# The orders of all five engines made anew in a transformer block of two gated FFNs around an attention step

## The reference

```python
x = x + 0.5 * ffn(layernorm(x))
x = x + attn(layernorm(x))
x = x + 0.5 * ffn(layernorm(x))

# ffn, hidden width 512, weights w*, h* ternary (-1, 0, 1)
h = silu(x @ w1.T * w1_s) * (x @ w2.T * w2_s)
h = gelu(h @ h1.T * h1_s)
h = gelu(h @ h2.T * h2_s)
y = h @ w3.T * w3_s

# attn, with a second layer norm of its own (gamma, beta)
keys = h @ Wk.T + bk;  values = h @ Wv.T + bv
w = exp((keys @ Wka.T + bka) / sqrt(128))
w = w / cumsum(w, axis=1)
out = cumsum(w * keys, axis=1) * values
```

## Time and profile before

| what | us |
|---|---|
| median of 3 runs (range) | 367.62 (367.56 to 367.99) |
| span of the profiled execution | 366.2 |
| median less that span (start and end outside it) | 1.4 |
| PE busy | 359.0 (98% of the span) |
| DVE busy | 319.5 (87%) |
| ACT busy | 283.6 (77%) |
| POOL busy | 171.9 (47%) |

### The profile page before, as it was taken

One profiled execution on the slowest core, in us unless ns is written; L12 is line 12 of the kernel. 1 busy time (PEld: TensorE's weight loads), 2 busy tenths in 40 slices (PEclk: granted clock), 3 DMA queues, 4 the chain that ended last, 5 costly groups with the idle time before them and its releaser, 6 DMA issues.

```text
span 366.2 us, 5192 instructions
## 1 busy us (share of the span) xinstructions
PE 359.0 (98%) x1572; PEld 284.6 (78%) x1572; DVE 319.5 (87%) x542; ACT 283.6 (77%) x463; POOL 171.9 (47%) x259
## 2 busy tenths in 40 slices
PE   7999999999999999999999999999999999999995
PEld 2678888778877887887878787887878877888885
DVE  5999788989989989999999989999999799947742
ACT  5898777886897789777876969868888796777763
POOL 3583375694124578512794545663574740520000
PEclk9999999999999999999999999999999999999999
DMA  7725504042000302100221021022024010050001
GB/s 255 242 96 167 166 2 115 0 113 62 1 2 0 99 18 58 59 4 0 56 63 57 3 58 59 0 59 58 0 60 117 1 57 2 0 143 2 30 1 59
DMA packets 17534, 21.44 MB, mean 59 GB/s; under 512 B 7392, under 2 KB 8672, under 8 KB 17248
## 3 DMA queue, kind: packets, MB, share of 16 engines
q1 hardware_dynamic: 16640, 20.15, 19.9%
q10 hardware_dynamic: 864, 0.93, 0.8%
HBM read 18.89 MB, written 2.19 MB: 58 GB/s over the span
## 4 chain that ended last, share of the span: by engine, by line
PE 97%; DVE 1%; ACT 0%; issue 0%; POOL 0%; POOLq 0%; DVEq 0%
PE hid_ps L654 62%; PE gate_ps L654 8%; PE y_ps L654 8%; PE up_ps L654 7%; PE y_ps L673 2%; PE xt_ps L847 2%; PE xt_ps L843 2%; PE xt_ps L850 2%; PE y_ps L763 1%; PE up_ps L718 1%; PE gate_ps L718 1%; DVE full L1092 0%; PE xt_ps L654 0%; DVE gate L1080 0%; DVE xt_sb L1152 0%
## 5 line engine op out<-in xcount | busy, mean ns | idle before, releaser
L654 PE MATMUL hid_ps<-act_hi,hi_h 128*128 128x512 f32 (+1 forms) x368 | 146.5, 398 | 0.0
L654 PE MATMUL hid_ps<-act_lo,hi_h 128*128 128x512 f32 (+1 forms) x368 | 143.1, 389 | 0.0
L1102 DVE TENSOR_TENSOR act_lo<-full,act_hi 128x512 fp32r<-128x512 f32 x157 | 117.3, 769 | 20.9 <-ACT act_hi L918 17.7
L911 ACT ACTIVATE full<-hid_ps,vec 128x512 f32<-128x512 f32 x123 | 84.3, 686 | 53.3 <-PE hid_ps L654 36.9
L654 PEld LDWEIGHTS hid_ps<-act_lo,hi_h 128*128 128x128 f32 x368 | 69.2, 188 | 16.3 <-issue 1.4
L654 PEld LDWEIGHTS hid_ps<-act_hi,hi_h 128*128 128x128 f32 x368 | 69.2, 188 | 16.0 <-issue 1.4
L918 ACT ACTIVATE act_hi<-full 128x512 fp32r<-128x512 f32 x127 | 78.6, 628 | 1.6
L580 POOL TENSOR_TENSOR xnt<-xt_sb,wide 128x512 f32<-128x512 f32 x22 | 31.6, 1437 | 49.5 <-DMA wide<-rows 43.8
L654 PE MATMUL hid_ps<-act_hi_second,hi_h 128*128 128x512 f32 x128 | 52.1, 407 | 0.0
L654 PE MATMUL hid_ps<-act_lo_second,hi_h 128*128 128x512 f32 x128 | 50.0, 390 | 0.0
L894 ACT ACTIVATE tanh<-gate_ps,s_half 128x512 f32<-128x512 f32 x60 | 40.6, 682 | 8.9 <-PE gate_ps L654 8.8
(11 more groups left out here) (168 smaller groups left out, 542.7 us busy)
## 6 DMA issues: line engine op xcount, KB each, us to landing
wide<-rows SPq DMA_DIRECT2D x44, 256.0 KB, 3.7
out<-xt_sb SPq DMA_DIRECT2D x7, 256.0 KB, 3.1
raw_h<-h2t SPq DMA_DIRECT2D x4, 256.0 KB, 7.0
x_sb<-x SPq DMA_DIRECT2D x1, 1024.0 KB, 5.0
xt_sb<-xt SPq DMA_DIRECT2D x1, 1024.0 KB, 5.0
x_sb<-x SPq DMA_DIRECT2D x3, 256.0 KB, 5.5
raw_h<-h1t SPq DMA_DIRECT2D x2, 256.0 KB, 6.0
xt_sb<-xt SPq DMA_DIRECT2D x2, 256.0 KB, 4.1
```

The costliest lines, as they stand in the source:

```text
L654: mm = eng.matmul(ps, w, a, start=(first and n == 0), stop=(last and n == len(seq_) - 1))
L911: eng.activation(full23[m % 2][:, :], home23(n, T, m)[:, :], ACT.Gelu, scale=col("sh1" if n == 2 else "sh2", m)).then_inc(s_gelu[n], 1)
L1102: eng.tensor_tensor(act_lo[a][:, m, :], full[m % 2][:, :], act_hi[a][:, m, :].bitcast(F32), ALU.subtract).then_inc(s_lo[n], 1)
```

## The change

Only the tables change. The same items stand in them, each exactly once: 286 on PE, 441 on DVE, 436 on ACT, 87 on POOL and 51 on SP. No function, buffer or semaphore is touched, and `PE` in `START` stays as it was. Strings are now longer or empty because an item's step number no longer follows its tile. The diff, cut to the head and three further places:

```diff
@@ -30,15 +30,18 @@
-        "hi:w1 bits:w2 hi:w2 z vec:s1 0:t bits:h1.1 bits:h1.3 0:tanh.0 0:tanh.1 0:tanh.2 0:high1.0 0:high1.1",
-        "bits:h2.0 bits:w3 tanh.3 high1.2 z.0 z.1 high1.3",
+        "hi:w1 bits:w2 hi:w2",
+        "0:z vec:s1 t bits:h1.1 tanh.0 tanh.1 bits:h1.3 bits:h2.0 tanh.2 high1.0 high1.1 tanh.3 bits:w3 "
+        "high1.2 z.0 z.1",
     ),
     "DVE": (
-        "stats aggr veps bits:w1 norm.0 norm.1 flag:copy1 norm.2 bits:h1.0",
-        "t vec:scales bits:h1.2 stats flag:raise2 gate.0 gate.1 up.0 flag:copy2 up.1 low1.0 aggr gate.2 veps "
-        "up.2 bits:h2.1 gate.3 up.3 2:stats low1.3 bits:h2.2 flag:raise3 1:t 3:stats flag:copy3 0:low2.0 "
-        "1:gate.0 0:low2.1 1:gate.1 1:up.0 1:up.1 0:low2.2 0:low2.3 1:low1.0 1:gate.2 1:low1.1 1:up.2 "
-        "1:gate.3 0:low3.0 2:t 1:up.3 1:low1.2 1:low1.3 0:low3.1 0:fold 0:low3.2",
+        "stats aggr veps bits:w1",
+        "0:norm.0 0:norm.1 0:norm.2 flag:copy1 bits:h1.0 vec:scales t bits:h1.2 stats gate.0 gate.1 "
+        "flag:raise2 up.0 flag:copy2 up.1 low1.0 aggr gate.2 veps up.2 gate.3 2:stats up.3 bits:h2.1 "
+        "bits:h2.2 low1.3 3:stats 1:t flag:raise3 flag:copy3 0:low2.0 0:low2.1 1:gate.0 1:gate.1 1:up.0 "
+        "1:up.1 0:low2.2 0:low2.3 1:low1.0 1:low1.1 1:gate.2 1:gate.3 1:up.2 1:up.3 0:fold 0:low3.0 0:low3.1 "
+        "2:t 1:low1.2 1:low1.3 2:gate.0 2:up.0 2:gate.1 0:low3.2 2:up.1 0:low3.3 1:low2.0 2:low1.0 2:low1.1 "
+        "2:gate.2 0:dt",
     ),
 }
 
@@ -46,143 +49,156 @@
 SECOND_LAYER = (
...
-    "p2dhi.1 p2bhi.2 p2dlo.1 p2dhi.2 p2dhi.3 flag:sum3 p1.0 p2dlo.2 p2dlo.3 p1.1"
+    "p2dhi.1 p2bhi.2 p2dlo.1 p2dhi.2 p2dhi.3 flag:sum3 p1.0 p1.1 p2dlo.2 p2dlo.3"
...
-        "park wide",
-        "park wide",
-        "a0:park a0:wide park wide",
-        "a1:park a1:wide park wide",
...
+        "park 3:park",
+        "",
+        "2:wide 3:wide a0:park",
...
-        "p1.0 p1.1 p4 p2.0 p2.1 u a4:values p2.2 p1.2 p2.3 a5:logits p1.3 12:u p3.0 a5:keys p3.1 p3.2 p3.3",
...
+        "a4:keys 10:p1.0 10:p1.1 p3.2 p3.3 9:p2.0 9:p2.1 a4:values 8:p4 10:p1.2 11:u 10:p1.3 a5:logits 12:u "
+        "9:p2.2 9:p2.3 a5:keys",
+        "p3.0 p3.1 p3.2 p3.3 a5:values 11:p1.0 11:p1.1",
...
-        "low2.0 low2.1 low2.2 low2.3 low3.0 dt low3.1 low3.2 last:dt.0 last:dt.1",
...
+        "15:gate.3 15:up.3 14:low3.0 14:low3.1 15:low1.3 14:low3.2 14:low3.3 low2.0 low2.1 low2.2 low2.3 "
+        "low3.0 low3.1 low3.2 dt last:dt.0 last:dt.1",
```

More of the change, by code:

```diff
@@ L52 @@
     "SP": (
-        "park wide",
-        "park wide",
-        "a0:park a0:wide park wide",
-        "a1:park a1:wide park wide",
-        "park wide",
-        "a2:park park a2:wide wide",
-        "a3:park a3:wide park wide",
-        "park wide",
-        "a4:park a4:wide park wide",
-        "a5:park a5:wide park wide",
-        "park wide",
-        "a6:park a6:wide park wide",
-        "a7:park 8:store 9:store a7:wide park wide",
-        "park 10:store 11:store store wide",
-        "store",
-        "store",
+        "park 3:park",
+        "",
+        "2:wide 3:wide a0:park",
+        "",
+        "",
+        "a0:wide",
+        "4:park 4:wide a1:park 5:park a1:wide 5:wide 6:park 6:wide a2:park 7:park",
+        "a2:wide 7:wide a3:park a3:wide 8:park 8:wide park wide a4:park 10:park a4:wide 10:wide",
+        "a5:park a5:wide 11:park 8:store 11:wide 12:park",
+        "12:wide",
+        "a6:park a6:wide 13:park",
+        "9:store store wide a7:park",
+        "",
+        "a7:wide 14:park",
+        "14:wide 11:store 15:park 15:wide",
+        "12:store 13:store store",
     ),
     "POOL": (
-        "hi:h2.0 hi:h2.1 norm hi:h2.2 hi:h2.3 3:norm xn.0 xn.1",
-        "hi:w3 xn.0 xn.1",
-        "a0:norm norm a0:xn.0 a0:xn.1 xn.0 xn.1",
-        "a1:norm norm 6:norm a1:xn.0 a0:weight a1:xn.1 xn.0 xn.1",
-        "xn.0 a0:dt xn.1",
-        "a1:weight a2:norm norm a2:xn.0 a2:xn.1 xn.0 xn.1",
-        "a3:norm a1:dt a2:weight norm a3:xn.0 a3:xn.1 xn.0 xn.1",
-        "a2:dt norm a4:norm a3:weight xn.0 xn.1",
-        "norm a4:xn.0 a4:xn.1 xn.0 xn.1",
-        "a3:dt a5:norm a4:weight a5:xn.0 a5:xn.1 norm a4:dt xn.0 xn.1",
-        "norm a5:weight xn.0 xn.1",
-        "a6:norm a6:xn.0 a6:xn.1 a5:dt norm a6:weight a7:norm xn.0 xn.1",
-        "a6:dt a7:xn.0 a7:xn.1 norm xn.0 xn.1",
-        "a7:weight a7:dt norm xn.0 xn.1",
-        "",
-        "",
+        "norm",
[16 rows of a table added]
     ),
     "PE": (
[17 rows of a table removed]
[23 rows of a table added]
     ),
     "ACT": (
[41 rows of a table removed]
[43 rows of a table added]
     ),
     "DVE": (
[35 rows of a table removed]
[39 rows of a table added]
     ),
```

## The result

| | kernel before | changed kernel |
|---|---|---|
| median of the comparison on record | 367.81 us (4 runs) | **377.16 us** (4 runs) |
| its runs | 367.56 to 369.0 | 374.68, 375.2, 379.13, 379.79 |
| ratio, 95% interval | | 1.0247, [1.0185, 1.0308] |
| the same kernel again, run 6 below | 367.62 (17 runs) | 373.78 (372.37 to 374.24, 5 runs) |
| its ratio, 95% interval | | 1.0151, [1.0127, 1.0175] |

The change makes the kernel 1.5 to 2.5% slower: about 6 us in ordinary executions, and 11 to 12 us in some. The profiled execution took 379.13 us, its span 377.3, so it is one of the long ones. Of the nine runs, seven lie between 372.4 and 375.2 and two at 379 to 380.

A forecast was written before the change was run, and what follows sets the result against it. The prediction took PE's own rate as the bound, DVE second. Terms 0 + 0.1 + 0.2 + 0 = +0.3 on the 366.2 us span gave 366.5, plus 1.4 to the median 367.9, stated as 367.8 us; range 367.0 to 369.3.

The forecast's parts named there:

- What bounds the kernel: From first `p3.0` to half-width end, PE's own work fills 328.0 to 329.5 of 331.0 us; DVE is second.
- fewer collisions, 0: DVE's `lo` subtractions: at best 13.2 us of DVE time go, but gain on the path 0 to 0.6, taken as 0.
- The head, +0.1, bounds to +0.6: Start up to `p3.0` of tile 0: 0.3 lost, 0.29 gained, 0.1 for copies; +0.1 us, bounds -0.3 and +0.6.
- the last three copies until about 26.8: POOL in the head: weight copies done about 26.8 us, so `p3.0`, at 26.83 before, costs 0 to 0.2.
- SP in the head, 0: Tile 2's reads wait behind tile 3's park near 25.0 us, but were issued then before too: cost 0.
- The middle, +0.2: Later third-layer starts, PE waiting for `act_lo`: +0.2 us, bounds from 0.6 us of waits vanishing to 3.8 us lost.
- a wait of 0.25: Third layer of tile 9: only the keys product separates `p2.3` and `p3.0`, so PE waits 0.1 + 0.15 us.
- My upper bound, 3.8 us: The middle's upper bound: all 15 later third-layer starts pay 0.25 us each.
- DVE falls behind in the attention stretch: Slower rival: paired order makes DVE late, 0.3 us for each of eight attention steps, 2.4 us, 370.2; chance 0.24 with milder forms.
- The end, 0: `dt` of tile 14 ends near 360.8, before `last:dt.0` at 362.08: cost 0, bounds 0 and +0.5 us.
- marks for being wrong: PE waiting over 1.5 us for DVE/ACT after 27 us, head over 0.7 off 26.83, or time falling over 0.7 with PE's work unchanged.

The follow-up runs named there:

- run 6: The changed kernel measured again, unedited: 373.78 us median of five runs (372.37 to 374.24).
- run 17: Kernel before, with GpSimd's two wide instructions per normalized tile on 4 columns from each buffer's second use: 367.79 us against 367.44, ratio 1.0009.
- run 1: Changed kernel, with SyncE's read for attention tile 4 (`a4:wide`) moved ahead of the park of tile 10: 374.24 us, ratio 1.0178.
- run 18: Changed kernel, with GpSimd's two wide instructions per normalized tile on 4 columns from each buffer's second use: 370.63 us.
- run 19: Changed kernel, with VectorE's reciprocals of attention tiles 1 to 7 on 4 columns each: 374.68 us.
- Run 15: The kernel of run 1 plus three VectorE order moves, and ScalarE's 23 gelu, gelu, high, high groups reordered to gelu, high, gelu, high: 373.49 us.
- run 8: The kernel of run 1, with VectorE's four reciprocals of attention tiles 3 and 4 on 4 columns each: 371.96 us.
- run 2: Changed kernel, with the whole SyncE table of the kernel before: 377.33 us.

## Why the prediction was wrong

Forecast 367.8 (367.0 to 369.3); 377.16 in the comparison, 373.8 in the ordinary executions.

- *What bounds the kernel*: right. PE's own rate, DVE second. And *fewer collisions, 0*: right as a gain. The mean fell to 739, and run 17 shows that in the kernel before even 716 is worth nothing. But those that are left cost time once VectorE has no slack: 3.48 us for two subtractions in run 1, and 3.1 us for the same cut in run 18. The Trainium skill (Perfetto Trace Analysis, Identifying the Most-Contended Engine) gives the busy time of the weight loads as one of two measures for TensorE; by it DVE's 87% outranked PE's 78%, which pointed to a gain. The measurement decides against it here.
- *The head, +0.1, bounds to +0.6*: it was +1.1. The step of this part that failed is "the last three copies until about 26.8". `low1.3` came at 19.59, where I had 19.5, but on GpSimd the norms took 3.2 and 3.45 us instead of 3.05 and the three copies 2.2 us instead of 1.8, and the last ended at 27.88. VectorE had two-operand instructions beside them; that these are the reason was not tested. I had taken durations from a stretch with another neighbour and left no slack between them.
- *SP in the head, 0*: right. The read of tile 2 goes out at 26.17 in run 6 and at 25.82 before: the norm of tile 3, whose park it waits for, ends at 25.73 there, 1.1 us earlier than before. But the step looked at one place only. A queue served in order with a park ahead of a read had to be checked along the whole table: at `a4:park 10:park a4:wide 10:wide` it is the worst single place of the change, 2.3 us with VectorE relieved (run 19) and more where the norm is late.
- *The middle, +0.2*: the step that failed most. From the first `p3.0` to PE's last product it is 338.96 us in run 6 (27.94 to 366.90) and 335.05 before (26.83 to 361.88): +3.9 in the fastest execution, where I had +0.2. At tile 9 I forecast a wait of 0.25 and there is one of 0.45, but for another reason than the pairs on ScalarE: I counted from the keys product and left out the logits ahead of it, which keep ScalarE for 3.3 us with their tables. Run 15 took the pairs apart and the wait stayed 0.46. I took +0.2 "since both tables space these points alike" without walking the VectorE table past tile 9. My upper bound, 3.8 us, was near what the ordinary executions lose after the head, and I let it go. What the runs show in place of this term is above all VectorE late in 190 to 225 us: taking 6.6 us of work off it there gives back 2.3 us (run 8), and taking GpSimd's wide work and its collisions away gives back 3.1 (run 18).
- *The rival "DVE falls behind in the attention stretch"*, 2.4 us with a chance of 0.24, is the right mechanism at about the right price (2.3 us in run 8), and it was too low in chance. Its argument against was wrong: collisions that go elsewhere do not give VectorE back its time where it is needed. In run 6 VectorE is busy for all of 190 to 220 us:

```profile
190.00:200.00 10.00, 10.00 (x43) 7.81 (x42) 10.00 (x15) 6.47 (x12) 6.15 (x5) 1.00 0.38 107
200.00:210.00 10.00, 9.52 (x42) 7.33 (x41) 10.00 (x18) 9.41 (x15) 4.47 (x10) 1.00 0.00 0
210.00:220.00 10.00, 10.00 (x43) 7.69 (x43) 10.00 (x14) 7.15 (x13) 5.46 (x5) 1.00 0.22 54
```

  Before, it had 1.8 of these 30 us idle; and from 120 to 150 us, where it was busy for 28.1, it is now busy for 23.2. The new order pushes VectorE's work from a stretch with room into one with none.
- *The end, 0*: right. From the start of the last product to the end it is 3.7 us in run 6 (before 4.3), and `dt` of tile 14 stands 2.1 us ahead of `last:dt.0`.
- Two of the marks for being wrong came true: PE waits over 1.5 us for DVE or ACT after 27 us, 2.77 at the logits of tile 4 alone in the long execution, and the head ends 1.1 us off 26.83, more than 0.7.

## What to carry to other kernels

When the bounding engine is at 98% and its helpers' orders were fitted to it, a new order has little to win: price it by the slack of each helper at each point of contact, and walk every in-order queue from end to end for an item that stands ahead of one that is ready. A second engine that is 94% busy has no slack in the places where it is 100% busy; look at it in windows of 10 us, not of 100. And before working on a cost, take it away by force (run 17): what brings nothing when it is gone will bring nothing when it is reduced, in that kernel. The answer holds for the order in which it was asked: the same cut was worth 3.1 us in the changed kernel (run 18).

## What the runs showed of the hardware

- A GpSimd instruction of 4 columns, which reads SBUF, was held for 4.35 us by seven VectorE instructions with two SBUF operands in a row. It is seen in one trace. In run 2 the same norm met the same train, and three of its instructions got in between, in 0.68, 0.61 and 1.29 us (the last, the root, takes 1.04 alone). The Trainium skill (SBUF — State Buffer, SBUF: two separate sides) says that of a VectorE instruction with two SBUF inputs and a GpSimd instruction that reads SBUF, the one that starts second blocks until the first is through. For single pairs the traces agree (a subtraction of 0.69 us takes up to 1.78); here the block lasted over a whole train, so a waiting GpSimd instruction did not get its turn behind the first of them.
- After nine microseconds in which PE was busy for 5.44, the granted clock averaged 0.57 for four, mostly the 1.2 GHz level: from the start of the logits product to that of the fifth matmul of 512 columns behind the transposes it was 3.94 us, and 2.34 in run 6 at a clock of 1.00, so these idle stretches cost 1.6 us more.
- ScalarE's change of tables is 1.28 us, twice for each logits product: 2.56 us around 0.69 us of work. The Trainium skill (ScalarE: Activation LUTs, What ACT_TABLE_LOAD costs) gives 1283 ns for the load, which the rows confirm, and 1380 ns of drain besides; here the next instruction starts 0.02 us after the load.
